# Turning the token shares in steps 6 and 8 of a block attention, on one core of Trainium2

## The reference, cut to what matters

```python
# block attention: 16 heads of 16 columns, blocks of 32 keys, the own block and the best 3 earlier ones
km = k.reshape(B, nblk, CHUNK, H, d).mean(axis=2)
gate = jnp.einsum('bshd,bnhd->bhsn', q, km)      # a future block -1e30, the own block +1e30
vals, idx = jax.lax.top_k(gate, TOPK)
scores = jnp.where(sel_tok & causal, jnp.einsum('bihd,bjhd->bhij', q, k) * d ** (-0.5), NEG)
o = jnp.einsum('bhij,bjhd->bihd', _softmax(scores), v)
# experts: 8 low-rank ones over shared weights, 2 for each token
rw, sel = jax.lax.top_k(_softmax(x @ Wg.T), K)
rw = rw / rw.sum(axis=-1, keepdims=True)         # the shares of a token
for k in range(K):
    x2 = jax.nn.silu(base1 + lora1) * (base3 + lora3)
    out = out + (x2 @ W2.T + lora2) * rw[:, k:k + 1]
```

## Time and profile before

| | before |
|---|---|
| median of 3 executions | 701.42 us (701.11 to 702.13) |
| the profiled execution | 701.29 us, its span 699.1 us |
| granted TensorE clock | 1.0 of full speed |
| busy: PE, DVE, ACT, POOL | 671.0, 489.0, 424.3, 297.8 us |
| chain that ended last | PE 76%, DVE 14%, ACT 6%, issue 3%, POOL 1% |
| block attention, steps 0 to 31 | about 408 to 493 us |

### The profile page before, as it was taken

One profiled execution on the slowest core, in us unless ns is written; L12 is line 12 of the kernel. 1 busy time (PEld: TensorE's weight loads), 2 busy tenths in 40 slices (PEclk: granted clock), 3 DMA queues, 4 the chain that ended last, 5 costly groups with the idle time before them and its releaser, 6 DMA issues.

```text
span 699.1 us, 13847 instructions
## 1 busy us (share of the span) xinstructions
PE 671.0 (96%) x4756; PEld 581.7 (83%) x4756; DVE 489.0 (70%) x1418; ACT 424.3 (61%) x1099; POOL 297.8 (43%) x301
## 2 busy tenths in 40 slices
PE   6999999999999999999999989999989999999997
PEld 3777888888889898887787855666889999999997
DVE  6798877877877787777786886777465555644544
ACT  3766168788797878888663788888654213222221
POOL 0584154546464555542164318998334410400000
PEclk9999999999999999999999999999999999999999
DMA  8902044453535444351910000200300000000000
GB/s 329 346 1 98 1 130 121 165 166 112 168 116 165 129 152 126 101 159 59 365 79 1 1 1 2 107 1 3 121 1 1 1 1 16 2 16 1 1 16 16
DMA packets 26725, 59.43 MB, mean 85 GB/s; under 512 B 3146, under 2 KB 12748, under 8 KB 26272
## 3 DMA queue, kind: packets, MB, share of 16 engines
q1 hardware_dynamic: 23584, 50.35, 21.5%
q0 software_dynamic: 3072, 8.20, 3.6%
HBM read 48.24 MB, written 10.49 MB: 84 GB/s over the span
## 4 chain that ended last, share of the span: by engine, by line
PE 76%; DVE 14%; ACT 6%; issue 3%; POOL 1%; DMA 0%; DVEq 0%; ACTq 0%
PE bank L2253 11%; PE bank L2020 7%; PE bank L1954 6%; PE bank L2302 5%; PE bank L2011 5%; PE bank L2276 5%; PE bank L2040 4%; PE bank L1961 3%; PE bank L2031 3%; PE bank L2082 3%; PE bank L2316 2%; PE bank L2222 2%; PE bank L2206 2%; PE bank L1894 2%; PE bank L2161 2%
## 5 line engine op out<-in xcount | busy, mean ns | idle before, releaser
L1062 ACT ACTIVATE sb<-bank,sb 128x256 f32<-128x256 f32 x128 | 59.6, 471 | 40.6 <-DVE sb L1558 33.4
L1558 DVE TENSOR_REDUCE sb<-bank 128x2 f32<-128x512 f32 x64 | 43.7, 683 | 47.5 <-PE bank L2020 47.1
L1264 ACT ACTIVATE h_parts<-sb 128x256 fp32r<-128x256 f32 x56 | 23.4, 418 | 71.3 <-DVE sb L1809 43.4
L2020 PE MATMUL bank<-sb 128*128 128x256 f32 x256 | 66.2, 381 | 0.0
L1800 DVE TENSOR_TENSOR sb<-sb,bank 128x256 f32<-128x256 f32 x56 | 23.5, 419 | 58.1 <-ACT sb L1227 58.1
L2253 PE MATMUL bank<-rounded,b_hi 128*128 128x256 f32 x224 | 63.1, 282 | 0.0
L2253 PE MATMUL bank<-rounded,b_lo 128*128 128x256 f32 x224 | 62.9, 281 | 0.0
L2253 PE MATMUL bank<-am_lo,b_hi 128*128 128x256 f32 x224 | 62.9, 281 | 0.0
L1227 ACT ACTIVATE sb<-bank 128x256 f32<-128x256 f32 x56 | 21.5, 383 | 62.4 <-PE bank L2253 62.4
L834 POOL DMA_INDIRECT expert_out<-sb x32 | 33.0, 1032 | 61.0 <-DVE sb L1500 44.6
L1069 ACT ACTIVATE sb<-sb 128x256 f32<-128x256 f32 x128 | 57.7, 503 | 0.1
(11 more groups left out here) (321 smaller groups left out, 1969.9 us busy)
## 6 DMA issues: line engine op xcount, KB each, us to landing
sb<-in_w_gate_up SPq DMA_DIRECT2D x32, 368.0 KB
sb<-in_w_down SPq DMA_DIRECT2D x32, 256.0 KB
sb<-in_w_pair SPq DMA_DIRECT2D x8, 704.0 KB
expert_out<-sb SPq DMA_DIRECT2D x1, 4096.0 KB, 23.7
sb<-expert_out SPq DMA_DIRECT2D x8, 512.0 KB, 6.3
sb<-in_w SPq DMA_DIRECT2D x1, 1792.0 KB, 13.8
sb<-in_b SPq DMA_DIRECT2D x1, 1792.0 KB, 8.1
sb<-in_sw_up SPq DMA_DIRECT2D x1, 1536.0 KB, 9.4
```

The costliest lines, as they stand in the source:

```text
L1062: act.activation(probs[:, u % 4, q, :], bank[3 + u % 2][:, q * S:(q + 1) * S], ACT.Exp, scale=-1.0, bias=row_min[:, u % 4, q:q + 1], accum ...
L1558: dve.tensor_reduce(row_min[:, u % 4, :], bank[3 + u % 2][:, :].rearrange("p (q n) -> p q n", q=QT), AX.X, ALU.min).then_inc(at_min, 1)
L2020: mm = pe.matmul(bank[3 + u % 2][:, q * S:(q + 1) * S], qb[i][:, h, b * S + q * P:b * S + (q + 1) * P], keys[:, h, b * S:(b + 1) * S], sta ...
```

## The change

- TensorE turns share groups 2 and 3 in steps 6 and 8 instead of 3 and 4, into banks 2 and 7. Each waits for `bl_o` (heads_out(n - 2) done, so that the bank is free) instead of share_out. In the steps behind them, 7 and 9, values1 is issued after the two turns and waits for the share's copy.
- ScalarE copies the groups in steps 1, 2, 6 and 8, between even_probsT and the second exponentials of the step.
- own_queries(1) stands with own_queries(0) ahead of the fills, no longer in step 2.
- share_rep lies in columns B3_AT on, over tables, instead of in region 2. So POOL's two copies also wait for blk_step 3 (L1756 has read its table), and POOL's splits of b13, which write over it, also wait for the fourth share group.

```diff
-SCORE_BANK, SHARE_BANK = (3, 4, 0, 1), (2, 7, 7, 7)
+SCORE_BANK = (3, 4, 0, 1)
+SHARE_AT = {6: 2, 8: 3}
...
-        share_rep = Strip(region2, phase + 3 * NT * D, 2 * NT * P).take(2 * NT, P)
+        share_rep = Strip(sb, B3_AT, 2 * NT * P).take(2 * NT, P)
...
             pool.wait_ge(r1_step, 10 + 2 * NT)
+            pool.wait_ge(blk_step, 3)
             for k in range(2):
                 pool.tensor_copy(share_rep[:, k * NT:(k + 1) * NT, :], along(share[:, :, k], (2, P))).then_inc(r1_share, NT)
...
             pool.wait_ge(ab_in, 48)
+            pool.wait_ge(fill_mm, len(fills()) + 4)
...
             act.wait_ge(qkT_out, NT)
-            own_queries(0)
+            for G in range(2):
+                own_queries(G)
...
                     even_probsT(2 * j - 2)
+                if j in (1, 2):
+                    share_out(j - 1)
+                if j in SHARE_AT:
+                    share_out(SHARE_AT[j])
...
                     exponents(2 * j + 1)
-                if 0 < j < 5:
-                    share_out(j - 1)
-                if j % 4 == 2 and j // 4 + 1 < GROUPS:
+                if j % 4 == 2 and 1 < j // 4 + 1 < GROUPS:
                     own_queries(j // 4 + 1)
...
                 pe.wait_ge(r1_share, 4 * n + 4)
-                pe.wait_ge(fill_out, len(fills()) + (n if n > 1 else 0))
+                if n < 2:
+                    pe.wait_ge(fill_out, len(fills()))
+                else:
+                    pe.wait_ge(bl_o, n - 1)
                 for i in range(4):
-                    mm = pe.transpose(bank[SHARE_BANK[n]][:, i * P:(i + 1) * P], share_rep[:, 4 * n + i, :], ident)
+                    mm = pe.transpose(bank[2 + 5 * (n % 2)][:, i * P:(i + 1) * P], share_rep[:, 4 * n + i, :], ident)
...
                     shares(1)
-                if j in (3, 4):
-                    shares(j - 1)
                 if j == 5:
-                    pe.wait_ge(fill_out, len(fills()) + 4)
-                if j % 2 and j > 2:
+                    pe.wait_ge(fill_out, len(fills()) + 2)
+                if j in SHARE_AT:
+                    shares(SHARE_AT[j])
+                behind_shares = j - 1 in SHARE_AT
+                if j % 2 and j > 2 and not behind_shares:
                     values1((j - 3) // 2)
                 if 0 < j <= 2 * QUADS:
                     probs1_turn(2 * j - 2)
                     probs1_turn(2 * j - 1)
+                if behind_shares:
+                    pe.wait_ge(fill_out, len(fills()) + SHARE_AT[j - 1] + 1)
+                    values1((j - 3) // 2)
```

More of the change, by code:

```diff
@@ L1207, in share_out @@
                 act.wait_ge(fill_mm, len(fills()) + n + 1)
-                act.activation(shareT[:, n // 2, n % 2 * CH:(n % 2 + 1) * CH], bank[SHARE_BANK[n]][:, :], ACT.Copy)\
+                act.activation(shareT[:, n // 2, n % 2 * CH:(n % 2 + 1) * CH], bank[2 + 5 * (n % 2)][:, :], ACT.Copy)\
                     .then_inc(fill_out, 1)
```

## The result

The changed kernel takes **703.35 us** (median of 22 runs, 700.3 to 706.78), the kernel before 701.25 (22 runs beside them on the same chip, 700.02 to 702.19). The ratio is 1.0024, with a 95% interval of 1.0013 to 1.0034: slower, by 2.1 us, and outside the range of the prediction.

The account below looks back on a forecast made before the run. TensorE, busy for 96% of the span, was taken as the bound. A gain of 1.76 us in the attention less 1.44 us from POOL's copies gave 0.32 faster: 701.1 us from 701.42, range 699.4 to 702.5.

Parts of the forecast that it names:

- Part 1: own_queries(1), 0.80 us of ScalarE, leaves step 2 for a 2.61 us queue wait near 393: costs nothing.
- Part 2: Block attention steps 1 to 5 replayed: step 6 starts at 423.08 instead of 426.12, 3.04 us gained.
- Part 3: Attention steps 6 to 10, with the moved share groups: 1.76 us of the gain stays, bounds 1.0 and 2.0.
- Rival C: Attention: stalls only move, as moved share groups wait for heads_out or late values hold quad_out; 701.4 us, chance 0.05.
- Part 4: POOL's share copies run beside VectorE's compares from 401.2: 2.04 us lost less 0.60 freed, first minimum 1.44 later.
- Rival A: At the share copies, POOL stands still rather than VectorE, or one copy collides: 699.1 or 700.1 us, chance 0.25.
- rival B: At 401 to 410, copies delay the first minimum by 2.04 us and the gain is only 1.0: 702.5 us, chance 0.15.
- Sum: Whole kernel: 1.76 us gained less 1.44 lost, 0.32 us faster, 701.1 us from the median of 701.42.
- What would show it: Signs in the trace: first minimum at 411.9, idle before first turn 2.1 us, step 2 to 6 about 10.0 us.
- After the attention nothing else binds: Behind the attention: POOL's 6.67 us to spare covers its delay, and feed-forward steps simply follow the attention's end.

Follow-up runs that it names:

- both fills: Changed kernel plus 12 unused transposes on TensorE ahead of the first turn and 14 unused matmuls ahead of feed-forward hidden step 5: 700.24 us, ratio 0.9988.
- a fill elsewhere: Changed kernel plus 14 unused matmuls on TensorE in the 2.10 us wait ahead of feed-forward hidden step 5: 702.4 us, ratio 1.0008.
- half a fill: Changed kernel plus 6 unused transposes on TensorE ahead of the first turn, leaving 1.10 us idle: 701.71 us, ratio 1.0.

## Why the prediction was wrong

**Part 1** (queries early, cost nothing): right, shown by the edit alone in before.

**Part 2** (3.04 us gained from step 2 to step 6): right, 3.01. The forecast of 10.0 us for the stretch was measured as 9.99, and the minimum that had waited for own_bias no longer does; its wait is now 0.71, for the scores.

**Part 3** (11.5 us from step 6 to 10; bl_o met; the second turn of step 9 waits for its exponential; the period stays): right, 11.51, with a stall of 0.56 at 434.44, and no wait on bl_o. Of 3.01 us, 1.68 stays; forecast 1.76. Rival C, that the stalls only move, is out.

**Part 4** (copies beside the compares, first minimum 1.44 later): the mechanism right, the size off. The 0.60 came free, but the compares lost 1.68, not 2.04, so the minimum came 1.07 later, at 411.50 instead of 411.9. The copies took 2.29 for 2.04: POOL bore a part. By the rule of the Trainium skill (SBUF — State Buffer, Who interferes with whom) such a pair excludes each other; this trace agrees for the greater part. The compares (1.54) and the copies (2.04) are 3.58 us of work by themselves, and both were done within the compares' 3.22 us. So 0.36 us ran side by side, and by that the forecast of 2.04 was too high. Rival A (POOL stands still) was right only for that quarter of a microsecond; rival B's 2.04 did not come, and its time of 702.5 is near the result for a reason that it does not contain.

**Sum**: 1.68 less 1.07 is 0.61 us faster, forecast 0.32; with both fills in place 0.5 was measured. Neither of the prediction's own signs of being wrong came: the first minimum is not before 410.5, and step 2 to step 10 takes 21.50 us, not over 22.2. The waits were forecast rightly, and the time was not.

**The step that failed** is the one that the sum left out: Part 4 let "everything from the first minimum on" be "shifted by it", and "What would show it" even named TensorE's idle of 2.1 us ahead of the first turn as a sign of being right. That idle time was priced at its length. It has a second price: 8 of 12 executions on one chip and 14 of the 22 on the first have a mean clock of 0.993 or less and took at least 2.6 us more than the one at 1.00, and with the idle time filled none of 24 does. In the three profiles that caught the loss behind this wait (the changed kernel with a fill elsewhere and with half a fill, and before with the new wait) the granted clock was at 0.50 for 7 to 17 us, which took 1.6 to 7.2 us. The sentence "After the attention nothing else binds" left out the same thing at the 2.10 wait, worth about 1 us in the changed kernel (701.44 and 700.46 us in its two profiles, with it and without). No term, no bound and no rival had the clock, so the range ended at 702.5 and the time was 703.35. The trace of before could have raised the question: its waits of 0.67, 1.27 and 2.10 all stood at a granted clock of 1.00, and the change lengthened the first to a value between them.

Shown: the new wait alone brings the loss (in before), keeping TensorE at work removes it (in after, on two chips), half the work leaves a median about half way (701.71 between 703.19 and 699.71, with intervals that overlap), and another place for the shares removes it at its root. The Trainium skill (TensorE: Matmul & The Clock Gate, HAM oscillation) tells that idle time of TensorE between bursts puts the clock back to its lower level; these traces agree in that. They differ in the length: the page speaks of longer idle times, and here 1.10 to 2.10 us were enough, in a part of the executions. The measurements decide.

**Left open**: why one execution loses the clock and the next, with the same 1.75 us, does not; why it comes back after 3, 7 or 17 us; and where the kernel before loses it, which about a quarter of its own executions do (10 of 35 on the last chip are at 0.993 or 0.995, with 701.83 us or more) and no profile of it caught; the 1.27 wait is the likely place. The length of an idle time is not all that counts either: 1.10 us ahead of the first turn came with the loss in 5 of 12 executions, 1.26 us ahead of the third share group in none of 11 (before with the early queries), and what else matters was not tried.

## What to carry to other kernels

Price idle time of the engine that bounds the kernel twice: once by its length, and once by what the granted clock does behind it, which a trace that happens to keep 1.00 does not show; so look at the clock and the time of every execution, not at the profiled one alone. When a buffer gets a new place, ask what its writer must now wait for and what that puts it beside: a copy that was of no hurry came to lie beside VectorE's work with two SBUF inputs, just ahead of the only thing that TensorE waited for. A wait that is worth nothing in one kernel may be worth its full length in the next, once the wait that covered it is gone, so edits that go together are tried together as well as alone.

## What was not expected of the hardware

- The granted clock fell to 0.50 at or behind idle times of 1.10, 1.26, 1.75, 1.77 and 2.10 us of TensorE, with the work around them f32 transposes of 128x128, scores of 32 rows, or (at 2.10) matmuls of 128x256; with 0.44 and 0.46 us ahead of the first turn none of 24 executions on two chips was at 0.993 or less. The same idle time gave executions with and without it: with 1.75 us one profile is at 1.00 throughout.
- It stayed low for some 3 us (at the 2.10, and behind the 1.26), some 7 (within 413 to 421 behind 1.77, 414.5 to 421.2 behind 1.10) and 17 us (415 to 432, behind 1.75). In the last, TensorE was busy for all of the 17 us and still was not given more.
- Half the clock did not double the time. Doubling would make 17 us at 0.50 cost 8.5 and 7 us cost 3.5; they cost 7.2, and 1.6 and 2.5. Eight scores took 1.65 us for 0.92, and in the 7 us a part fell on waits that were there anyway.
- Two POOL copies of 1.02 us beside seven compares with two SBUF inputs cost VectorE 1.68 us and POOL 0.25, with 0.36 us of their work side by side; a POOL copy of 1.04 beside minima with one SBUF input cost neither anything (0.28 us for the minimum, as alone).
